# Adaptive FFN with low rank on one Trainium2 core: who forms the pair and weight sums of the first down projection, and where the low-rank product of the fourth pair stands

## The reference

```
# condition FFN with low rank (x: 8 x 128 x 512, F = 1376, rank 16), lora_indices per batch row
def lora_add(base, inp, A, B):
    t = einsum('bri,bni->bnr', A[layer][idx], inp)
    return base + einsum('bor,bnr->bno', B[layer][idx], t) * 0.5
gate = lora_add(x @ W_gate.T, x, A_gate, B_gate)
up   = lora_add(x @ W_up.T,   x, A_up,   B_up)
act  = silu(gate) * up
down = lora_add(act @ W_down.T, act, A_down, B_down)
# second FFN (I = 1792) on the RMS-normalised result, and the residual
nx = down * rsqrt(mean(down^2) + eps) * ln_w
out = x + (silu(nx @ gate_w.T) * (nx @ up_w.T)) @ down_w.T
```

## Time and profile before

| | us |
|---|---|
| median of 3 runs | 413.83 (413.66 to 415.65) |
| profiled execution, its own time | 414.94 |
| its span, first to last instruction | 412.9 |
| PE busy | 393.1 (95%) |
| DVE busy | 346.1 (84%) |
| ACT busy | 252.3 (61%) |
| POOL busy | 47.0 (11%) |

### The profile page before, as it was taken

The page is one execution under the profiler, slowest core; times in us unless marked ns, Lnnn a source line. Parts: engine busy times, 40 slices in busy tenths (PEclk is TensorE's granted clock), DMA queues, the critical chain, the costliest instruction groups (busy, mean ns, idle before and its releaser), DMA issues.

```text
span 412.9 us, 5738 instructions
## 1 busy us (share of the span) xinstructions
PE 393.1 (95%) x1954; PEld 324.7 (79%) x1954; DVE 346.1 (84%) x475; ACT 252.3 (61%) x390; POOL 47.0 (11%) x34
## 2 busy tenths in 40 slices
PE   9999999999996993699989999999999999999997
PEld 5999888888874782588858788888888888888886
DVE  4799987777588889989999988787787869899994
ACT  5879786767666387387365554655556567375730
POOL 6300000000155149213000000000000000000000
PEclk9999999999998898699989999999999999999999
DMA  7530263111587593400020113131212123205112
GB/s 261 176 124 6 75 171 104 51 50 44 198 182 193 181 228 64 112 4 0 0 104 0 52 52 102 51 103 51 103 52 102 48 93 120 121 2 193 51 51 102
DMA packets 15517, 38.96 MB, mean 94 GB/s; under 512 B 2434, under 2 KB 4994, under 8 KB 15490
## 3 DMA queue, kind: packets, MB, share of 16 engines
q1 hardware_dynamic: 13360, 32.19, 23.0%
q0 software_dynamic: 1008, 4.59, 6.3%
q10 hardware_dynamic: 1122, 1.84, 1.3%
HBM read 36.51 MB, written 2.10 MB: 94 GB/s over the span
## 4 chain that ended last, share of the span: by engine, by line
PE 83%; DVE 10%; issue 4%; ACT 3%; DVEq 0%; ACTq 0%
PE bank L1605 48%; PE bank L1968 16%; PE bank L1860 5%; PE bank L1823 3%; PE bank L1777 3%; DVE xs L1074 3%; PE bank L1812 3%; PE bank L1615 2%; DVE ws L1074 2%; ACT xs L540 1%; PE bank L1718 1%; PE bank L1771 1%; DVE last_wd L1074 1%; DVE down_w L1074 1%; DVE wsum L1086 1%
## 5 line engine op out<-in xcount | busy, mean ns | idle before, releaser
L1605 PE MATMUL bank<-xs,ws 128*128 128x512 f32 x840 | 198.7, 394 | 2.7 <-DVE mu L1133 1.7
L1605 PEld LDWEIGHTS bank<-xs,ws 128*128 128x128 f32 x840 | 158.0, 190 | 37.2 <-DVE mu L1133 2.4
L540 ACT ACTIVATE xs<-act 128x512 fp32r<-128x512 f32 (+1 forms) x73 | 50.1, 703 | 38.5 <-PE bank L1860 10.4
L1074 DVE TENSOR_TENSOR xs<-act,xs 128x512 fp32r<-128x512 f32 (+1 forms) x66 | 54.2, 839 | 3.0 <-ACT xs L540 2.4
L1074 DVE TENSOR_TENSOR ws<-wraw,ws 128x256 fp32r<-128x256 f32 (+2 forms) x45 | 32.2, 718 | 14.4 <-ACT ws L540 14.3
L540 ACT ACTIVATE bank<-bank 128x512 f32<-128x512 f32 x34 | 19.4, 578 | 38.4 <-PE bank L1605 33.2
L1074 DVE TENSOR_TENSOR ws<-wsum,ws 128x1024 fp32r<-128x1024 f32 x20 | 28.2, 1409 | 16.6 <-ACT ws L540 16.6
L1860 PE MATMUL bank<-xs,down_w_sums 128*128 128x512 f32 x120 | 30.4, 410 | 9.5 <-DVE xs L1074 9.5
L540 ACT ACTIVATE mu<-bank 128x512 f32<-128x512 f32 x44 | 26.1, 596 | 21.7 <-PE bank L1605 16.1
L1968 PE MATMUL bank<-xs,vs 128*128 128x512 f32 x168 | 38.2, 389 | 0.0
L1968 PEld LDWEIGHTS bank<-xs,vs 128*128 128x128 f32 x168 | 31.5, 188 | 6.5
(11 more groups left out here) (146 smaller groups left out, 509.7 us busy)
## 6 DMA issues: line engine op xcount, KB each, us to landing
wraw<-wgu_in SPq DMA_DIRECT2D x22, 512.0 KB, 3.3
down_w_sums_raw<-wc_in POOLq DMA_DIRECT2D x7, 640.0 KB, 8.5
wdr<-vs_in SPq DMA_DIRECT2D x7, 512.0 KB, 3.3
wraw<-vj_in SPq DMA_DIRECT2D x3, 896.0 KB, 4.7
down_w_sums_raw<-wc_in SPq DMA_DIRECT2D x4, 640.0 KB, 5.0
down_w_raw<-wc_in SPq DMA_DIRECT2D x3, 640.0 KB, 4.3
xa<-xT_in SPq DMA_DIRECT2D x4, 256.0 KB, 4.2
xa<-xT_in ACTq DMA_DIRECT2D x2, 512.0 KB, 5.2
```

Source lines behind the costliest of these rows:

```text
L540: return nc.scalar.activation(out_ap, in_ap, ACT.Copy, scale=scale)
L1074: return nc.vector.tensor_tensor(out_ap, raw, v32(part), ALU.subtract)
L1605: ins = mm(z[:, :], w_slot(j)[:, w, s, k * P:(k + 1) * P], xs[:, c, r, k, :], start=(start and k == 0 and s == 0 and r == 0), stop=(k == 1 ...
```

## The change

The change has five parts.

- The pair sums T3, T2 and T4 are formed by adding DMAs from SBUF to SBUF (`add_act`), issued by POOL; T1 is a subtraction on DVE (`t1`). T2 now has the parts (0, 1), (2, 3), and the waits of `hi_c` follow.
- The weight sums of tiles G1+1 to G1+3 come from three DMAs each: SP loads a base (`load_base`, new input `wbase_in`) into `wsum`, POOL adds further blocks from HBM (`two_w`, new input `wmore_in`, 384 KB) and then adds one sum to two others inside SBUF (`more_w`, 256 KB). The DVE and POOL instructions for them go.
- The call `t_c(range(6, 8))` (low rank of the fourth pair) moves from group 7 to behind C11, and C11 has two items ahead of `p4` in place of one. `hi_b` and `lo_b` of tile G1 move from group 7 to behind CT2's operands.
- SP loads `raw10` before the weights of CT4, C22 and CT1, and C22's before CT1's.
- On ACT and DVE several steps change places: among them `hi_w10(1)`/`lo_w10(1)` now stand behind the operands of CT4, `hi_w(C22)` ahead of its operands, and `square_hi` ahead of the copy of X21.

Core of the diff:

```diff
@@ SP
             load_down_w(C21, 0, 1)
-            sp.wait_ge(s_p3, S1)
-            load_down_w(CT4, 1, 1)
-            sp.wait_ge(s_p4, S1)
-            load_down_w(CT1, 1, 1)
-            load_down_w(C22, 0, 1)
             sp.wait_ge(s_c22f, S1 // 2)
...
+            sp.wait_ge(s_p3, S1)
+            load_down_w(CT4, 1, 1)
+            sp.wait_ge(s_p4, S1)
+            load_down_w(C22, 0, 1)
+            load_down_w(CT1, 1, 1)
+
+            def load_base(j):
+                sp.wait_ge(s_wblo, j - 2)
+                sp.dma_start(wsum[:, :, :], wbase_in[j - G1 - 1].rearrange("p (a m) -> p a m", a=4)).then_inc(s_wbase, 16)
+
+            load_base(G1 + 1)
             load_w(G1 + 2)
+            load_base(G1 + 2)
             load_w(G1 + 3)
+            load_base(G1 + 3)
@@ POOL
-            def pair_sum(to, more, op=ALU.add):
-                nc.gpsimd.tensor_tensor(to, to, more, op).then_inc(s_tp, 1)
...
+            def add_act(n, to, more):
+                if n >= 2:
+                    pool.wait_ge(*t_added(n - 2))
+                nc.gpsimd.dma_start(to, more, accum_op=ALU.add).then_inc(s_t_add[n % 2], 16)
+
+            def two_w(j):
+                n = j - G1 - 1
+                pool.wait_ge(s_wbase, 16 * n + 16)
+                nc.gpsimd.dma_start(wsum[:, 0:3, :], wmore_in[n].rearrange("p (a m) -> p a m", a=3), accum_op=ALU.add
+                                    ).then_inc(s_wadd, 16)
+
+            def more_w(j):
+                pool.wait_ge(s_wadd, 32 * (j - G1 - 1) + 16)
+                nc.gpsimd.dma_start(wsum[:, 2:4, :], wsum[:, 1:2, :].to_broadcast([P, 2, 256]), accum_op=ALU.add
+                                    ).then_inc(s_wadd, 16)
@@ ACT, DVE: which sum an operand waits for
-                    a.wait_ge(*((s_tp, T2_0 + n) if n < 3 else (s_last, 2)))
+                    for added in ((T2_01,), (T2_01, T2_23), (T2_23,), ())[n]:
+                        a.wait_ge(*t_added(added))
+                    if end == KC:
+                        a.wait_ge(s_last, 2)
...
+            def t1(n):
+                k, end = C_PARTS[CT1][n]
+                v.wait_ge(s_clo, KC * CT2 + end)
+                for half in range(k // 2, (end - 1) // 2 + 1):
+                    v.wait_ge(*t_added(T4_01 + half))
+                part = act_c(k, end, 0)
+                nc.vector.tensor_tensor(part, part, act_c(KC + k, KC + end, 1), ALU.subtract).then_inc(s_t1, 1)
@@ ACT, order in the down projection
+            hi_c(CT3, 0)
+            hi_c(CT3, 1)
+            hi_a(G1 + 1)
             hi_c(CT3, 2)
+            hi_w(CT4, cw_loaded(CT4))
             hi_b(G1 + 1)
-            hi_w(CT1, cw_added(S1_21))
             for n in range(3):
                 hi_c(CT4, n)
+            hi_w10(1)
...
+            square_hi()
             a.wait_ge(s_nx, 4)
             hi_x(1, X21, nx0[:, 2:4, :])
-            square_hi()
@@ PE
                         t_c_of_pairs(2)
                         t_c(range(6))
-                    elif j == S1 - 1:
-                        t_c_of_pairs(3)
-                        t_c(range(6, 8))
...
                 c_item(k)
-                if k == 0:
+                if k == 1:
                     p4(S1 - 1)
             t_c_of_pairs(S1 // 2)
             pe.wait_ge(s_act_pad, 1)
+            t_c(range(6, 8))
             t_c(range(8, FC))
```

More of the change, by code:

```diff
@@ L194, in build @@
         C11, CT2, C21, CT3, CT4, CT1, C22 = range(7)
-        CW_ORDER = (C11, CT2, CT3, C21, CT4, CT1, C22)
+        CW_ORDER = (C11, CT2, CT3, C21, CT4, C22, CT1)
         CW_HI = (C11, CT3, CT2, C21, CT4, CT1, C22)
@@ L534, in _ @@
-            pool.wait_ge(s_wsum, 3 * g + 2)
-            nc.gpsimd.tensor_tensor(wsum[:, 3, :], wsum[:, 2, :], raw_w[:, 2, :], ALU.add).then_inc(s_wsum, 1)
+            for j in range(G1 + 2, G1 + 4):
+                two_w(j)
+                more_w(j)
         @block.scalar
```

177 lines of the change are left out of this document (85 added, 92 removed).

## The result

| | before | after |
|---|---|---|
| median, us | 414.27 (413.66 to 415.65, 4 runs) | 420.96 (420.48 to 421.04, 4 runs) |
| ratio to before, 95% interval | | 1.0145 (1.012 to 1.0171) |
| span of the profiled execution | 412.9 | 419.1 |

The change makes the kernel 6.7 us slower; the forecast was 5.4 us slower, 419.2. In the spans the loss is 6.2 us. Of these 0.35 stand there at 101 us already, ahead of everything that was changed (PE's row of 24 matmuls starts at 101.47, before at 101.12).

A forecast was written before the change was run, and what follows sets the result against it. PE was taken as the bound, busy 393.1 of 412.9 us. Losses of 3.8 at short_c and 1.9 of clock, less 0.3 in the norm, gave 5.4 slower: 419.2 us from 413.83, range 409 to 424 (8 in 10).

The forecast's parts named there:

- First part: Up to C11's end: DVE no longer stretched, waits at C11 and p4 gone; C11 ends near 136.0, 7.5 us ahead.
- Second part: C11 to CT3: three DMAs in a row delay CT2 to 153.4 from 144.9; the 7.5 us gain shrinks to 0.9.
- rival 3: Loads and short runs hurt more: all 5.8 us of loads delay T2, landing at 152.8; total 423 us; chance 0.13.
- My price per MB inside SBUF: Adding DMAs inside SBUF taken at the HBM add's 5.9 us per MB, plus 2.1 us fixed each.
- The 4.4 us on ACT: Between T2 and CT2: two CT2 operands, G1's sums, C21's weights and one seed copy, 4.4 us with overlap.
- Third part: At short_c: w10's second half waits behind T4 of tile 4 (177.9); short_c 3.8 us later, PE idle 4.7 before it.
- The clock term: Behind the wait at short_c: PE runs slow at low clock, between 0 and 1.9 us lost, 1.9 taken.
- The rest: After short_c: removed POOL and DVE weight sums worth nothing, t1 hidden, square_hi saves 0.3 us in the norm, second FFN untouched.
- Rival 1: Adds inside SBUF cost as little as plain transfers (2.95 us per MB), undisturbed by loads; total 407.4 us; chance 0.22.
- Rival 2: POOL's DMA queue does not bound w10, so only CT3's end counts; total 412.6 us; chance 0.17.
- Rival 4: C11 still waits, so the count of s_t comes up to 4 us later; total 423 us; chance 0.05.
- Both marks: Forecast wrong if T2 of tiles 2, 3 lands under 8 us after s_t's count, or T4 of tile 4 before 174.

The follow-up runs named there:

- the measurement of prices: A separate kernel computing nothing of the reference, timing single DMAs and DVE subtractions: adds inside SBUF of 256, 512, 768 KB took 3.3, 4.5, 5.7 us.
- the move alone: Kernel before, with the fourth pair's low rank behind C11, p4 behind two items and some neighbours reordered, POOL's sums kept: 420.44 us, ratio 1.0122.
- the first repairs: Changed kernel with the fourth pair's low rank back in group 7 (416.22 us), w10's second half ahead of CT4's operands (417.83), or both (414.19).
- the four later ones: Both orders undone, G1+1's sums behind T4: 416.6 us; then T3 by POOL: 414.07; then more adds behind T4: 417.54; then T3 by DMA, loads behind T2: 421.62.
- the loads behind T2: Changed kernel, but SP loads the weights of CT4, C22 and CT1 only after T2 of tiles 2, 3 landed: 417.74 us, ratio 1.0071.
- the last kernel: Kernel with more adds behind T4 and T3 by POOL, with G1+1 to G1+3's weight sums back on DVE and POOL: 407.83 us, ratio 0.9824.

## Why the prediction was right, point by point

| step | forecast | measured |
|---|---|---|
| C11 ends | 136.0 | 135.8 |
| second count of s_t | 137.1 | 137.1 |
| T3 of tile 3 lands | 140.8 | 145.1 |
| T2 of tiles 2, 3 lands | 149.0 | 151.4 |
| CT2 starts | 153.4 | 155.7 |
| CT3 ends | 176.2 | 179.0 |
| T4 of tile 4 lands | 177.9 | 179.1 |
| `short_c` starts, later than before | 3.8 | 5.4 |
| slow rows behind it | 1.9 | 2.8 |
| norm | -0.3 | -2.2 |
| sum | 5.4 | 6.0 (spans 6.2, medians 6.7) |

- **First part.** Right to 0.2 us, and each wait that was named went. DVE is back at 1.2 us per 1024 columns, and the measurement of prices shows that a sum of POOL does this to it (3.1 us lost to a sum of 4.4). The wait at C11 goes with the place of `lo_b(G1)`, as the prediction has it, and not with POOL: where POOL forms T3 again but `lo_b(G1)` stands late, C11 does not wait; where POOL forms T3 and `lo_b(G1)` stands in its old place (the move alone), it does (2.7).
- **Second part.** The mechanism is shown: moving the low rank back brings CT2 10.3 us forward, and moving it alone costs 1.2% without any DMA. The mis-sized term is the share of SP's loads. I put 2 us of up to 5.8 on T2 and none on T3; T3 took 8.0 us, and 3.9 without the loads, and with what follows they cost 5.7 up to CT2. This is rival 3's mechanism, and it is real. My price per MB inside SBUF was too high (5.9 against 4.6), which is 1.7 us too much for T3 and the two T2 (1.31 MB). So the loads and the rest were 4.1 us too low and the price 1.7 too high, and that 149.0 came within 2.4 of 151.4 is in part luck.
- **The 4.4 us on ACT** between T2 and CT2 measured 155.7 - 151.4 = 4.3.
- **Third part.** The wait is there, 3.5 for 4.7, behind w10 as forecast. T4 of tile 4 landed 1.2 later than forecast, but again out of two errors. `two_w` landed at 164.3 and not at 160.8, 2.4 of it since all before it was late. The six DMAs behind it took 14.9 us and not 17.1, which is near what the measured prices give (15.2, with 4.6 per MB for the four adds inside SBUF and 6.1 for the two from HBM). That it is a chain of its own and not a consequence of CT2 is shown by the run where CT2 came 10.3 earlier and 7.8 were lost here. The clock term was 2.8 for 1.9: I took the loss of one row of 30 and it was two rows, `short_c` (1.33) and CT4 (1.53).
- **The rest.** The norm gave 2.2 where I had 0.3: the wait shrank by 1.1, and rows behind it were no longer slow, 1.4. I had costed the order of `square_hi` and forgotten that a wait also costs the rows behind it, though I had used that rule two paragraphs earlier. Which of the moved steps shortened this wait was not tried; the place of the low rank is not it, since with that move alone the wait is 1.7 again.
- **Rival 1** fell on both legs: an add inside SBUF is not as cheap as a plain transfer (4.6 against 1.5 inside SBUF and 2.6 from HBM), and loads disturb it, in the measurement of prices by their full time. By the Trainium skill, page "DMA: Bandwidth & Descriptors", section on the anatomy of one DMA from GpSimd, it would be 2.3 us per MB, an estimate from its rate, which is near the plain transfer from HBM (2.6); the runs do not agree for adds. The prediction's own ratio of an add to a plain transfer (5.9 against 2.95, a factor of 2) was too low as well: from HBM it is 2.3, inside SBUF about 3. **Rival 2** fell with the wait at `short_c`. **Rival 4** fell too: C11 has no wait.
- Both marks that would have made the forecast wrong stayed away: T2 landed 14.3 us after the count (not under 8), T4 of tile 4 at 179 (not before 174).

What I got wrong lay behind the forecast. The three expectations for the first repairs were too low by 2 to 8 us, and the four later ones that put weight sums or adds behind T4 by 8 to 16 us. Each time one wait was removed, and I did not ask who waits next for the same queue or the same buffer. Only the loads behind T2 and the last kernel came out in their ranges; the move alone lay 1.4 us above its own.
